# First attention in head pairs: two transposed chunks, two products with V and two score tiles at a time

## The reference, cut to what matters

```python
kv = jnp.concatenate([context, latents], axis=1)      # 512 + 256 = 768 rows for each batch
q = (latents @ Wq)...; k = (kv @ Wk)...; v = (kv @ Wv)...
q = rms_norm(q, q_norm_w); k = rms_norm(k, k_norm_w)
scores = jnp.einsum('bhgqd,bhkd->bhgqk', qg, k) * scale
probs = softmax(scores)
out = jnp.einsum('bhgqk,bhkd->bhgqd', probs, v)
x = x + tanh(g_xattn[0]) * (out @ Wo)
```

## Time and profile before

| | us |
|---|---|
| median of 3 runs | 985.45 (983.24 to 991.03) |
| the profiled execution, its time | 984.21 |
| its span in the trace | 982.4 |
| PE busy in the span | 949.6 (97%) |
| one turn of the loop (from one start of the transposes of the first queries to the next) | 88.83 |
| first attention, to its last product | about 731 |

### The profile page before, as it was taken

The page is one execution under the profiler, slowest core; times in us unless marked ns, Lnnn a source line. Parts: engine busy times, 40 slices in busy tenths (PEclk is TensorE's granted clock), DMA queues, the critical chain, the costliest instruction groups (busy, mean ns, idle before and its releaser), DMA issues. The chain is left out here.

```text
span 982.4 us, 18543 instructions
## 1 busy us (share of the span) xinstructions
PE 949.6 (97%) x6876; PEld 824.3 (84%) x6876; DVE 637.1 (65%) x1107; ACT 478.6 (49%) x937; POOL 352.9 (36%) x256
## 2 busy tenths in 40 slices
PE   6999999999999999999999999999999998999996
PEld 4889989998998899899989989998987876677755
DVE  6777557556754774675567457656744665888856
ACT  4466346535633653464356336534624612656634
POOL 2354325333631633344244316244114721080033
PEclk9989999999999999999999999999999999999999
DMA  6021103202120310032021102200015214933001
GB/s 235 2 76 30 48 1 86 64 0 62 35 53 0 86 60 4 0 94 55 0 75 22 53 0 86 86 0 11 23 42 196 88 40 133 224 64 60 2 1 43
DMA packets 40693, 55.01 MB, mean 56 GB/s; under 512 B 8656, under 2 KB 20560, under 8 KB 40656
## 3 DMA queue, kind: packets, MB, share of 16 engines
q1 hardware_dynamic: 40080, 54.49, 20.0%
q10 hardware_dynamic: 576, 0.00, 0.0%
HBM read 50.22 MB, written 4.26 MB: 55 GB/s over the span
## 5 line engine op out<-in xcount | busy, mean ns | idle before, releaser
L480 DVE TENSOR_TENSOR ptL<-tbank,ptH 128x512 fp32r<-128x512 f32 x192 | 132.2, 689 | 70.2 <-ACT ptH L322 67.8
L322 ACT ACTIVATE ptH<-tbank 128x512 fp32r<-128x512 f32 x192 | 115.5, 602 | 114.4 <-PE tbank L618 114.0
L618 PE MATMUL tbank<-ident,probs 128*128 128x128 f32 x860 | 132.2, 277 | 3.0 <-DVE ptL L480 2.7
L493 DVE TENSOR_REDUCE negmax<-score 128x1 f32<-128x768 f32 x128 | 120.4, 950 | 11.2 <-PE score L80 10.7
L343 ACT ACTIVATE probs<-score,negmax 128x768 f32<-128x768 f32 x128 | 115.5, 903 | 14.9 <-DVE negmax L493 14.9
L78 PE MATMUL obank<-ptH,vH 128*128 128x256 f32 x384 | 121.3, 316 | 0.0
L230 POOL TENSOR_TENSOR rnorm<-sumsq,neg_half 128x2 f32<-128x2 f32 (+1 forms) x80 | 71.4, 896 | 120.5 <-DVE sumsq L453 120.5
L451 DVE TENSOR_REDUCE sumsq<-probs 128x2 f32<-128x256 f32 (+1 forms) x80 | 42.0, 525 | 106.6 <-ACT probs L317 65.7
L618 PEld LDWEIGHTS tbank<-ident,probs 128*128 128x128 f32 x860 | 97.7, 141 | 13.2 <-DVE ptL L480 9.4
L80 PE MATMUL obank<-ptH,vL 128*128 128x256 f32 x384 | 108.8, 283 | 0.0
L79 PE MATMUL obank<-ptL,vH 128*128 128x256 f32 x384 | 108.2, 282 | 0.0
(11 more groups left out here) (282 smaller groups left out, 2240.9 us busy)
## 6 DMA issues: line engine op xcount, KB each, us to landing
wqo_stage<-in_wq SPq DMA_DIRECT2D x9, 1024.0 KB, 5.6
wqo_stage<-in_wo SPq DMA_DIRECT2D x8, 1024.0 KB, 6.9
factors<-r_scratch SPq DMA_DIRECT2D x32, 256.0 KB, 3.9
wkv_stage<-in_wkv SPq DMA_DIRECT2D x9, 512.0 KB, 6.4
a_qS<-q_scratch SPq DMA_DIRECT2D x24, 128.0 KB, 5.0
ctx_stage<-in_ctxT SPq DMA_DIRECT2D x2, 1024.0 KB, 7.1
kS<-k_scratch SPq DMA_DIRECT2D x32, 64.0 KB, 4.0
q_scratch<-qpart SPq DMA_DIRECT2D x16, 128.0 KB, 1.9
```

The source lines that it names most:

```text
L322: act.activation(out, tbank[c % 2][:], ACT.Copy, scale=scale).then_inc(t_hi, 1)
L480: i = dve.tensor_tensor(out, tbank[c % 2][:], f32(hi), ALU.subtract)
L493: dve.tensor_reduce(negmax[:, m:m + 1], score[m % 2][:, 0:SKV], AX.X, ALU.max, negate=True).then_inc(s_max, 1)
L618: i = pe.transpose(tbank[c % 2][:, n * P:(n + 1) * P], block_in, S.ident[:])
```

## The change

The unit is now a pair (`PAIRS = 4`, w = 2 * (head pair) + batch): 2 heads of one batch, with 4 score tiles and 6 chunks. A chunk is one block of keys for the 512 queries of both heads, again 4 transposes. `times_v` of a chunk is 3 products of 512 columns over the whole of `obank[w % 2]`. PE's order in a pair is: two transposed groups, (from the third pair on) the last two products with V of the pair before, two score tiles of the next pair, two transposed groups, two score tiles, two chunks with V, two transposed groups, two chunks with V. In the first pair the transposes of the queries 2 and 3 and the last two chunks with V follow; the last pair has no scores to compute and leaves its last two chunks to `finish_units`. ACT and DVE follow this order. On DVE `normalise_o` of the pair before stands behind the first two `lo` and ahead of the maxima; on ACT `hi_o` stands behind the first two `hi_p` and ahead of the exps.

`probs` has 8 slots in place of 4, and `k_rows` and `sq` lie in the later 4. `qTH` and `qTL` hold 2 heads, `factors` is one buffer (so its load waits for the `normalise_o` before), and `o_norm` lies in the last tile of `q_rows` (so `evac_q` of tile 3 waits for POOL's last `oTL`). Four score tiles of the next group, not two, stand between the output products. POOL waits for the fifth score tile, not the third, before it splits Wo. In the last group the heads 2 and 3 are multiplied with Wo by halves of the rows. In the prologue the projections of the last 4 blocks of K and V are cut in halves with scores and transposes between them.

```diff
-    NP, NPT = 4, 4
+    NP, NPT = 8, 4
...
-    o_norm, factors = sb("o_norm", [P, ROWS], fp32), sb("factors", [P, 2, ROWS], fp32)
+    o_norm, factors = q_rows[:, RT - 1, :], sb("factors", [P, ROWS], fp32)
...
-    U, CH = 2 * GRP, 3
+    PAIRS, CH = GRP, KVT
+    order = [("q", 0), ("k", 0), ("q", 1), ("k", 1), ("k", 2)]
+    for w in range(PAIRS):
+        for j in range(CH):
+            order.append(("p", CH * w + j))
+        if w == 0:
+            order += [("q", 2), ("q", 3)]
...
# sync
+                if h:
+                    sp.wait_ge(o_normed, GRP * g + h)
+                sp.dma_start(factors[:], r_dram[h].rearrange("q n -> (q n)").partition_broadcast(P)).then_inc(r_in, 16)
...
# scalar
+                for w in range(PAIRS):
+                    for half in range(CH // 2):
+                        for c in range(CH * w + 2 * half, CH * w + 2 * half + 2):
+                            hi_p(g, c)
+                        if half == 0 and w:
+                            hi_o(g, w - 1)
+                        if half < 2 and w + 1 < PAIRS:
+                            for m in range(4 * w + 4 + 2 * half, 4 * w + 6 + 2 * half):
+                                exp(g, m)
+                    if w == 0:
+                        hi_q(g, 2)
+                        hi_q(g, 3)
...
+                act.wait_ge(o_lo, GRP * g + GRP)
                 evac_q(g + 1, 3)
...
# vector
+                for w in range(PAIRS):
+                    reciprocals(g, w)
+                    lo_p(g, CH * w)
+                    lo_p(g, CH * w + 1)
+                    if w:
+                        normalise_o(g, w - 1)
+                    if w + 1 < PAIRS:
+                        for t in range(3):
+                            maximum(g, 4 * w + 4 + t)
+                    lo_p(g, CH * w + 2)
+                    if w + 1 < PAIRS:
+                        maximum(g, 4 * w + 7)
+                    for j in range(3, CH):
+                        lo_p(g, CH * w + j)
+                    if w == 0:
+                        lo_q(g, 2)
+                        lo_q(g, 3)
...
# tensor
+                if m >= 2:
+                    pe.wait_ge(s_exp, 16 * g + m - 1)
...
+            def times_v(g, c):
+                w, j = c // CH, c % CH
+                if j == 0 and w >= 2:
+                    pe.wait_ge(o_normed, GRP * g + w - 1)
+                pe.wait_ge(t_lo, TC * g + at["p", c] + 1)
+                key = (w % 2) * KVT + j
+                mm3(pe, obank[w % 2][:], (vH[:, key, :], vL[:, key, :]), (ptH[:, c % NPT, :], ptL[:, c % NPT, :]),
+                    j == 0, j == CH - 1).then_inc(pe_pv, 1)
...
+                for w in range(PAIRS):
+                    c = CH * w
+                    transpose_probs(g, w, 0)
+                    transpose_probs(g, w, 1)
+                    if w >= 2:
+                        times_v(g, c - 2)
+                        times_v(g, c - 1)
+                    if w + 1 < PAIRS:
+                        scores(g, w + 1, 0)
+                        scores(g, w + 1, 1)
+                    transpose_probs(g, w, 2)
+                    transpose_probs(g, w, 3)
+                    if w + 1 < PAIRS:
+                        scores(g, w + 1, 2)
+                        scores(g, w + 1, 3)
+                    times_v(g, c)
+                    times_v(g, c + 1)
+                    transpose_probs(g, w, 4)
+                    transpose_probs(g, w, 5)
+                    times_v(g, c + 2)
+                    times_v(g, c + 3)
+                    if w == 0:
+                        transpose_q(g, 2)
+                        transpose_q(g, 3)
+                        times_v(g, c + 4)
+                        times_v(g, c + 5)
...
+                for t in range(2):
+                    transpose_q(g + 1, t)
+                    transpose_k(g + 1, t)
                     output(g, t)
+                scores(g + 1, 0, 0)
+                scores(g + 1, 0, 1)
+                transpose_k(g + 1, 2)
+                output(g, 2)
+                scores(g + 1, 0, 2)
+                scores(g + 1, 0, 3)
+                output(g, 3)
```

More of the change, by code:

```diff
@@ L346, in attend @@
             def attend(g):
[L347 to L358, removed]
+                for w in range(PAIRS):
[10 more added lines that the diff above has]
+                        hi_q(g, 3)
             def prepare(g):
-                hi_q(g, 0)
-                for i in range(3):
+                for i in range(2):
+                    hi_q(g, i)
                     hi_k(g, i)
+                exp(g, 0)
+                hi_k(g, 2)
+                for m in range(1, 4):
+                    exp(g, m)
             def turn(g):
@@ L374, in turn @@
                 prepare(g + 1)
-                exp(g + 1, 0)
-                exp(g + 1, 1)
             def last():
@@ L388, in _ @@
                 evac_kv(0, c, True)
-            hi_q(0, 0)
-            hi_k(0, 0)
+            for i in range(2):
+                hi_q(0, i)
+                hi_k(0, i)
             evac_kv(0, EARLY, True)
-            hi_k(0, 1)
+            for m in range(3):
+                exp(0, m)
             evac_kv(0, EARLY + 1, True)
-            exp(0, 0)
+            exp(0, 3)
             hi_k(0, 2)
-            exp(0, 1)
             turns(act, turn, last)
@@ L503, in normalise_o, with lo_p @@
                 dve.wait_ge(r_in, 16 * (GRP * g + h + 1))
[L504 removed]
+                dve.wait_ge(pe_pv, 24 * g + CH * (h + 1))
                 if h:
                     dve.wait_ge(o_lo, GRP * g + h)
[L507 to L508 removed]
+                rows = [m.rearrange("p (n q) -> p n q", q=P) for m in (o_norm, obank[h % 2][:])]
+                dve.tensor_tensor(rows[0], rows[1], factors[:].rearrange("p (q n) -> p n q", n=RT),
                                   ALU.mult).then_inc(o_normed, 1)
+            def lo_p(g, c):
+                lo(g, ("p", c), ptL[:, c % NPT, :], ptH[:, c % NPT, :])
             def attend(g):
[L512 to L527, removed]
[L528 removed]
+                for w in range(PAIRS):
[15 more added lines that the diff above has]
+                        lo_q(g, 3)
             def add_out(g, t, bank):
@@ L542, in turn @@
                 add_out(g, 0, obank[0][:])
+                lo_q(g + 1, 1)
                 lo_k(g + 1, 1)
                 add_out(g, 1, obank[1][:])
+                maximum(g + 1, 0)
                 lo_k(g + 1, 2)
-                maximum(g + 1, 0)
-                maximum(g + 1, 1)
+                for m in range(1, 4):
+                    maximum(g + 1, m)
                 add_out(g, 2, obank[0][:])
@@ L594, in project_q, with project_kv @@
                 i.then_inc(pe_q, 1)
-            def project_kv(g, chunks=range(NKV), first=False):
+            def project_kv(g, chunks=range(NKV), first=False, parts=(0, 1)):
                 pe.wait_ge(wkv_split, NS * g + NS)
@@ L619, in transposes, with transpose_k @@
                 i.then_inc(pe_t, 1)
-            def transpose_k(g, i, first=False):
+            def transpose_k(g, i):
                 pe.wait_ge(normed, NIT * g + K_NORMED[i])
-                transposes(g, ("k", i), [k_tiles(2 * i + n // 2, first)[:, n % 2, :] for n in range(4)])
+                transposes(g, ("k", i), [k_tiles(2 * i + n // 2)[:, n % 2, :] for n in range(4)])
             def transpose_q(g, h):
@@ new lines, in scores, with transpose_probs @@
+                q = slice(b * SQ + (m % 2) * P, b * SQ + (m % 2 + 1) * P)
+                for k0, n in ((0, 512), (512, 256)):
+                    keys = slice(b * SKV + k0, b * SKV + k0 + n)
+                    i = mm3(pe, score[m % 2][:, k0:k0 + n], (qTH[:, h % 2, q], qTL[:, h % 2, q]),
+                            (kTH[:, keys], kTL[:, keys]), True, True)
+                i.then_inc(pe_s, 1)
+            def transpose_probs(g, w, j):
+                if j == 0:
+                    pe.wait_ge(s_exp, 16 * g + 4 * w + 4)
+                transposes(g, ("p", CH * w + j),
+                           [probs[:, (4 * w + n) % NP, j * P:(j + 1) * P] for n in range(4)])
@@ L684, in finish_units @@
             def finish_units(g):
-                for j in range(CH):
-                    times_v(g, U - 1, j)
+                for c in range(CH * PAIRS - 2, CH * PAIRS):
+                    times_v(g, c)
             def output(g, t):
```

144 lines of the change are left out of this document (51 added, 93 removed).

## The result

The changed kernel takes 1012.53 us (1012.04 to 1018.5, 4 runs), the one before 984.88 (983.24 to 991.03, 4 runs). The ratio is 1.031, interval 1.027 to 1.034: 3% slower. The forecast was 1009, its range 997 to 1019.

What follows compares the result with a forecast made beforehand. PE was taken to bound the kernel, busy 97% and waiting only 1.4 us a turn. Added waits +29.0, products with V -3.8 and prologue 0 made +25 on 984.2: forecast 1009 us, range 997 to 1019.

Steps and rivals of the forecast that it cites:

- The waits in a pair: In attention, PE waits at third score tiles, sixth groups, query tile and last pair: 4.85 us against 1.4 before.
- Cheaper products with V: In attention, 72 products of 512 columns replace 144 of 256: gain 0.48 us a turn, 3.8 in 8 groups.
- Pairing the transposes: Transposed groups on PE: two in a row cost as much as two apart, so no gain by itself.
- The projections: Between output products, the fourth transposed group adds 0.2 us a turn, 1.4 in 7; scores moved there cost nothing.
- The prologue: At the start, about 2 us idle, then 1.5 before the fifth score tile; taken as 0, bounds -2 and +2.
- Costed at nothing: Other added waits, evac_q on POOL's oTL, the one factors buffer, SP's queue, second normalise_o: room enough, no cost.
- POOL's room at the second `normalise_o`: Second pair's normalise_o needs the first oTL, behind POOL's split of Wq: 1.6 us of room.
- Rival 2: Order breaks even or gains, first maximum starting when its tile is done: 980.4, or 969 without waits; chance 0.12.
- The half case: Part of rival 2: half the added waits in attention, 995 us; chance 0.04, split over the bound.
- Rival 4: Weights late for POOL, so the second pair's normalise_o is late each time: 1014 us; counted within the forecast's 0.82.
- Rival 3: PE's clock falls after waits within turns, costing 2.5 us an attention, 20 in all: 1029 us; chance 0.06.
- The sum: Whole kernel: waits +29.0, products with V -3.8, prologue 0, together +25 us on the profiled 984.2.

Runs made afterwards that it cites:

- the fourth lo: Changed kernel with the fourth lo of a pair ahead of the maximum of the fourth new score tile on DVE: 1026.13 us, the turn 94.03.
- the two kernels without waits: Written-out mixed order with the first reciprocal of a group moved behind the first lo, products with V of 512 or 256 columns: 971.2 and 974.41 us.
- the two spread tiles: Changed kernel with factors and the third tile of q_rows used in turn, so a load waits for the normalise_o before the last: 1013.13 us.
- the kernel with the short maximum: Changed kernel with each maximum read over the first 256 of 768 columns of a score tile: 993.27 us.
- the written order: Changed kernel with attend reordered on PE, ACT and DVE, hardly anything by twos, 973.63 us; with the first reciprocal moved behind the first lo, 971.2 us.

## Why the prediction was right

- **The waits in a pair** (29.0 in the sum, the step that decides). Right in size, place and cause. Every place is within 0.1 us of its forecast, and the turn came out at 92.3 where the sum gives 88.83 + 3.45 - 0.48 + 0.2 = 92.0. The second pair's cause is shown by moving `normalise_o` (with the `hi_o` that waits for it), the last pair's by moving `hi_o`; their expectations, 1004.5 and 1003.5, were worked out in the same manner and met within 0.3 us, and so was the loss of the fourth lo (1026). The waits by kind were less even than "three times as long": 2.4 times for `ptL`, 7 times for the exps. That the order of before "gives waits of 1.5" by the same method is told without its working; its trace has 1.4.
- **Cheaper products with V** (-3.8). Right: 0.47 a turn between the two kernels without waits, 3.2 in the median, against 0.48 and 3.8. The two prices of the earlier trace rows carry over. The Trainium skill ("TensorE: Matmul & The Clock Gate", section "Wait — 56ns, not 53.3ns?") gives a fixed 2.5 ns for a product, by which I had estimated 0.19 a turn. The runs show a larger fixed part: 0.47 us over 72 products more is 6.5 ns.
- **Pairing the transposes** (0). No run gives it a gain: with hardly any pairs, a turn takes 87.0, the 86.9 of the same prices.
- **The projections** (+0.2 a turn). 0.3, of which one part was in the turn of before.
- **The prologue** (0, bounds -2 and +2). Right only as a bound, and the fall of the clock was mis-sized. The first turn starts 2.4 later than before. One attention of the six turns' kind is +3.4 of that, so the prologue gained 1.0, in a profile without a fall. In all ten experiments, with the same prologue, the clock did fall, for 3.4 us in three and for 6.8 in seven, which costs 0.7 and 1.9, by the time from the transposes of the queries 1 to those of the queries 2 in the four kernels that change nothing ahead of these. So the new prologue lies between 0.3 better and 0.9 worse than before. The prediction read 3.5 us of fall in the earlier trace rows; the trace of before has it from 49.5 to 56.3, 6.8 us. An idle stretch, which I had called the cause of a fall, was there both with and without one.
- **Costed at nothing.** The single `factors`: shown, by the two spread tiles. POOL's room at the second `normalise_o`: the first `oTL` ends at 172.5 in the changed kernel and `normalise_o` starts at 173.9, 1.4 us of room where I had 1.6. Rival 4 didn't happen; in the kernel with the short maximum the same wait did appear. The wait of `evac_q` wasn't tried alone; no wait shows there.
- **Rival 2** (break even or better). Its condition could not be met: the diff puts two `lo` ahead of the first maximum in DVE's queue. (The half case, 995, lies just below the range of 997 to 1019 that was said to hold it.) But the rival's floor was right: 969 "with none at all", and the written order reaches 971.2. What spoke against it was this order by twos, not the head pairs.
- **Rival 3** (the clock). 1.00 in the turns, also in the kernel with the longest waits (94.03 a turn). The falls that did occur, once in the prologue or once in the second attention, are a matter of 2 us.
- **The sum.** +25.2 forecast, 28.6 in the profile. The 3.4 between them: seven turns' worth of waits some hundredths longer each, 7 x 0.27 = 1.9; the last part 3.6 in place of 2.97, 0.7, which I haven't resolved further; the unchanged part 1.9, where this one profile has a fall of the clock; and the prologue -1.0, where it has none. That the last two nearly cancel is luck.

## What to carry to other kernels

Where engines keep their queues in order and two buffers alternate, don't ask how much an engine works but how long it is from the release of a buffer to its next use, with every instruction that stands in front of a link of that chain; write it down for each unit, since the first, second and last differ. An instruction that waits for something slow belongs behind those that hurry, and the one that feeds a slow round trip belongs first; here moving three instructions was worth 17 us, and the whole order 41. Before a late instruction is pulled forward, name what it pushes back: the fourth `lo`, meant to spare 0.4 a pair, cost 1.7 a turn net.

## What the runs showed that I had not expected

The same prologue, with the same 2.3 us of PE idle in 3.5, was followed by a fall of the clock to its lower level in all ten experiments (0.57 in the mean of 4 us with two spread tiles) and by none in the changed kernel's profile (1.00), which had a fall 840 us later instead, in code that no run changes. At the start the clock came up at 14.6 us in one profile and at 17.0 in another, worth 1.1 us. What decides between these cases no run shows. Whoever compares the starts of two profiles, or their unchanged parts, must look at the granted clock there first.

The load of the factors from DRAM held DVE up by 0.87 us in one turn and by 0.23 in the next, with the same instructions before it; over that profile it landed 3.0 to 6.0 us after its issue. A hand-over through DRAM needs its slack for the late case; with the first reciprocals 7.7 us earlier in the turn (19.9 us after its start in place of 27.6) all turns took 87.0.
